# A later wait point for the second product of super-block 0 in a macaron transformer layer

## The chip, the cores and the metric

The kernel runs on one Trainium2 chip, on all 8 cores, each with its own batch element (2048 tokens of 1024 features) and the same weights. The metric is the device time in microseconds of the slowest core, from its first to its last instruction, as one launch takes it. The cores don't exchange data.

## What is computed

The layer is a feed-forward block, attention, and the same feed-forward block again, each with a layer normalisation in front and a residual around it:

```python
x = x + 0.5 * ffn(layernorm(x))
x = x + attn(layernorm(x))
x = x + 0.5 * ffn(layernorm(x))

def ffn(x):                       # n = tokens, D = 1024, HIDDEN = 4096
    top1 = argmax(softmax(x @ gate_w.T))        # one of two routed experts
    masked = x[None] * one_hot(top1)            # per expert, the others' tokens zeroed
    h = relu(einsum('end,edh->enh', masked, w1) + b1[:, None])
    routed = (einsum('enh,ehd->end', h, w2) + b2[:, None]).sum(0)
    return routed + relu(x @ sw1 + sb1) @ sw2 + sb2   # and the shared expert
```

Attention has 16 heads and uses one projection for query, key and value.

## The kernel before

`build` writes out, in Python, one list of instructions per engine, with semaphore waits made explicit by a small class `Sched`. `sch.bump(sem, n)` counts how far a semaphore will have come when everything emitted so far has run; `sch.val(sem)` is that count; `sch.wait(engine, sem, value)` puts a wait in the engine's list, and puts none if the value is 0 or if that engine has waited for as much already. Each engine then runs its list strictly in order. VectorE counts DVE, ScalarE counts ACTs, TensorE counts MM.

Three segments follow one another: `emit_ffn` (first feed-forward stage), `emit_attn`, and `emit_ffn` again. Activations lie in SBUF as `x_sb`, features on the partitions, and are worked on in 4 strips of 512 tokens (`NSTRIP`, `TS`). The hidden units of the shared expert and of the two routed ones, 3 x 4096, are cut into 12 super-blocks of 1024 (`NSUP`, `HE`): super-blocks 0 to 3 are the shared expert, 4 to 7 and 8 to 11 the routed ones, on masked input. The weights of a super-block are loaded by POOL's DMA queue two super-blocks ahead, once the block two before has ended (`issue_next`).

For each super-block and strip there are two products:

- `do_mm1` (L534): 8 groups of 8 matmuls, 128x128 weights by 128x512 activations, at L556, alternately into the PSUM banks ps_a and ps_b. ScalarE takes each out at L566 with bias and ReLU into `ar_h`.
- `do_mm2` (L582): 8 groups of 8 matmuls at L593, from `ar_h`, alternately into ps_c and ps_d. VectorE takes each out by adding it to the residual in `x_sb`: at L606 in super-block 0 (with the bias), at L613 in the others. Ahead of each group TensorE waits at L586 for the eviction that last used this bank (`ps2_free`) or for the argument `mm2_extra`, whichever is later.

Super-block 0 (L622 to L635) is interleaved with the layer normalisation of the coming strips, which the other super-blocks find finished:

- `stage_stats` (L314), called as `sf`: TensorE sums x (L326) and squares made by ScalarE (L344, L353); VectorE takes both rows out (L335, L361).
- `stage_post` (L366), called as `pf`: a few row operations (L373, L378, L385), a matmul that spreads the scale over the partitions (L391), ScalarE's exponential (L397), a matmul that spreads the mean (L402), and then 16 operations of VectorE, for each of 8 feature blocks a subtraction (L411) and a multiplication (L415), which write the normalised strip `ar_ln`.
- `stage_gate` (L423), called as `gf`: the routing masks (L435 to L477).

The order in which super-block 0 hands work to the engines is, for strips 0, 1, 2, 3: `do_mm1` of the strip, statistics of strip + 2, `pf` of strip + 1, `do_mm2` of the strip, and from strip 2 on the gate of strip - 2. So on VectorE the 16 operations for the next strip stand ahead of the 8 evictions of this strip's second product, and on TensorE the matmul of L402 stands directly ahead of L593. Strip 3 has neither statistics nor `pf` ahead of its second product.

`xwait_dve`, the argument of this call before, is 0 in the first stage and, in the second, the last VectorE count of attention, which TensorE waits for already ahead of the statistics.

Of the kernel before, what the change touches and what calls it, by code (L numbers as in the profile page):

```python
# [68 lines left out]
def build(phases=("ffn1", "attn", "ffn2")):  # L69
# [15 lines left out]
    with es:  # L85
# [40 lines left out]
        sch = Sched()  # L126
        X, MM, ACTs, DVE, GP, OUT = "x", "mm", "act", "dve", "gp", "out"
# [34 lines left out]
        def w2blk(slot, hc, dc):  # L162
            o = slot * 8192 + hc * 1024 + dc * 128
            return ar_w2[:, o:o + 128]
# [335 lines left out]
        def emit_ffn(xwait_dve, wst, ps_d, ps_w, ps_w2, ps_e, ps_f):  # L500
# [81 lines left out]
            def do_mm2(sup, st, slot, mm2_extra):  # L582
                h_all = max(h_relu_tok)
                for dc in range(NKC):
                    pst = (ps_c, ps_d)[dc % 2]
                    sch.wait("tensor", DVE, max(ps2_free[dc % 2], mm2_extra))  # L586
                    if dc > 0:
                        sch.wait("tensor", ACTs, h_all)
                    for hc in range(NKC):
                        if dc == 0:  # L590
                            sch.wait("tensor", ACTs, h_relu_tok[hc])
                        def f2(t, S, _hc=hc, _dc=dc, _slot=slot, _pst=pst):
                            ins = t.matmul(_pst[:, :], w2blk(_slot, _hc, _dc),  # L593
                                           ar_h[:, _hc * TS:(_hc + 1) * TS],
                                           start=(_hc == 0), stop=(_hc == NKC - 1))
                            if _hc == NKC - 1:
                                ins.then_inc(S[MM], 1)
                        sch.emit("tensor", f2)
                    g2 = sch.bump(MM, 1)
                    sch.wait("vector", MM, g2)  # L600
                    sch.wait("vector", DVE, tok_b2)
                    o0 = dc * NT + st * TS
                    if sup == 0:
                        def fx(v, S, _dc=dc, _o0=o0, _pst=pst):
                            xsl = x_sb[:, _o0:_o0 + TS]
                            v.scalar_tensor_tensor(  # L606
                                out=xsl, in0=_pst[:, :],
                                scalar=b2sh[:, _dc:_dc + 1], in1=xsl,
                                op0=ALU.add, op1=ALU.add).then_inc(S[DVE], 1)
                    else:  # L610
                        def fx(v, S, _o0=o0, _pst=pst):
                            xsl = x_sb[:, _o0:_o0 + TS]
                            v.tensor_add(xsl, xsl, _pst[:, :]).then_inc(S[DVE], 1)  # L613
                    sch.emit("vector", fx)
                    stt_tok[dc][st] = sch.bump(DVE, 1)
                    ps2_free[dc % 2] = stt_tok[dc][st]
                    if pending_lnm:
                        pending_lnm.pop(0)()
                while pending_lnm:
                    pending_lnm.pop(0)()  # L620

            sf[0](); sf[1](); pf[0]()  # L622
            for st in range(NSTRIP):
                do_mm1(0, st, 0, 0)
                if st + 2 < NSTRIP:
                    sf[st + 2]()
                if st + 1 < NSTRIP:
                    pf[st + 1]()
                do_mm2(0, st, 0, xwait_dve)
                if st == 2:  # L630
                    ext["all_ln"] = max(ln_tok)
                if st >= 2:
                    gf[st - 2]()
# [338 lines left out]
        if do1:  # L972
            with nc.psum_tensor("ps_d1", [128, TS], F32) as ps_d1, \
                 nc.psum_tensor("ps_w1", [1, TS], F32) as ps_w1, \
                 nc.psum_tensor("ps_v1", [1, TS], F32) as ps_v1, \
                 nc.psum_tensor("ps_e1", [128, TS], F32) as ps_e1, \
                 nc.psum_tensor("ps_f1", [128, TS], F32) as ps_f1:
                for s0 in range(2):
                    wst1["w1"][s0] = issue_w1(s0, s0 % 2, 0, "f1")
                    wst1["w2"][s0] = issue_w2(s0, s0 % 2, 0)  # L980

                def issue_next_ffn1(sup):
                    nxt = sup + 2
                    tok = wst1["sup_last_mm"][sup]
                    if nxt < NSUP:
                        wst1["w1"][nxt] = issue_w1(nxt, nxt % 2, tok, "f1")
                        wst1["w2"][nxt] = issue_w2(nxt, nxt % 2, tok)
                wst1["issue_next"] = issue_next_ffn1
                xw, _, ffn1_mm = emit_ffn(0, wst1, ps_d1, ps_w1, ps_v1, ps_e1, ps_f1)
                if doa:  # L990
                    wready["wq"] = issue_wqut("q", wst1["sup_last_mm"][10])
            sch.seg_break()
# [23 lines left out]
        if do2:  # L1016
            with nc.psum_tensor("ps_d2", [128, TS], F32) as ps_d2, \
                 nc.psum_tensor("ps_w2", [1, TS], F32) as ps_w2, \
                 nc.psum_tensor("ps_v2", [1, TS], F32) as ps_v2, \
                 nc.psum_tensor("ps_e2", [128, TS], F32) as ps_e2, \  # L1020
                 nc.psum_tensor("ps_f2", [128, TS], F32) as ps_f2:
                if wst2["w1"][0] is None:
                    wst2["w1"][0] = issue_w1(0, 0, attn_mm, "f2")
                wst2["w2"][0] = issue_w2(0, 0, attn_mm)
                wst2["w1"][1] = issue_w1(1, 1, attn_mm, "f2")
                wst2["w2"][1] = issue_w2(1, 1, attn_mm)

                def issue_next_ffn2(sup):
                    nxt = sup + 2
                    tok = wst2["sup_last_mm"][sup]  # L1030
                    if nxt < NSUP:
                        wst2["w1"][nxt] = issue_w1(nxt, nxt % 2, tok, "f2")
                        wst2["w2"][nxt] = issue_w2(nxt, nxt % 2, tok)
                wst2["issue_next"] = issue_next_ffn2
                _, xtok, _ = emit_ffn(xw, wst2, ps_d2, ps_w2, ps_v2, ps_e2, ps_f2)
# [97 lines left out]
```

## Time and profile before

| | us |
|---|---|
| two timed runs | 4184.4 and 4484.0, median 4334.2 |
| profiled execution, as timed | 4184.9 |
| its span (slowest core) | 4183.2 |
| spans of the eight cores | 4177.3 to 4183.2 |
| TensorE matmuls busy | 3810.0 (91%) |
| ScalarE busy | 1223.3 (29%) |
| VectorE busy | 1133.8 (27%) |
| POOL busy | 48.6 (1%) |

The two timed runs are 7% apart, so the profiled execution, close to the lower one, is the one to which the rows belong. The busy times are shares of a span made of unlike stages. The first feed-forward stage begins at about 50 us, when the input has landed; super-block 0 runs to about 296 us, attention from about 1540 to 2685, and super-block 0 of the second stage from there to about 2930.

### The profile page before, as it was taken

How to read it: one execution, taken by the hardware profiler on the slowest of the kernel's cores; microseconds unless marked ns; L12 is line 12 of the kernel's file. 1: busy time of each engine (PE TensorE's matmuls, PEld its weight loads, DVE VectorE, ACT ScalarE, POOL GpSimd, SP SyncE). 2: the span in 40 equal slices, each digit the busy share in tenths (PEclk: the TensorE clock that was granted, in tenths of full speed). 3: DMA queues.
4: the chain of work that ended last, by engine and by line, in shares of the span. 5: the costliest groups of instructions: out<-in, count | busy, mean ns of one | idle time of the engine just before them, and what ended most of it. 6: DMA issues, size and time to landing. Idle time of an engine off the chain costs nothing. (4 is left out here: it accounts for less than half of the span.)

```text
span 4183.2 us, 45422 instructions; the slowest of 8 cores (4177.3 to 4183.2 us)
## 1 busy us (share of the span) xinstructions
PE 3810.0 (91%) x16624; PEld 1598.7 (38%) x16880; DVE 1133.8 (27%) x2179; ACT 1223.3 (29%) x2956; POOL 48.6 (1%) x67
## 2 busy tenths in 40 slices
PE   3789999999999996889888889877999999999998
PEld 0234444444444431233332333323344444444443
DVE  1331212233223325121231212234211232233222
ACT  1111112111221121666637666421122112211121
POOL 0000000000000000000000000000000000000000
PEclk8899999999999997556575565789999999999999
DMA  7002222222222100100001000300222222222202
GB/s 161 0 1 41 41 41 41 41 41 41 41 41 41 21 1 0 21 1 1 1 1 21 1 1 1 45 16 0 41 41 41 41 41 41 41 41 41 36 6 81
DMA packets 55268, 124.63 MB, mean 30 GB/s; under 512 B 1808, under 2 KB 1808, under 8 KB 53008
## 3 DMA queue, kind: packets, MB, share of 16 engines
q0 software_dynamic: 52144, 104.86, 16.1%
q1 hardware_dynamic: 2912, 16.85, 1.2%
q8 instruction: 144, 2.36, 0.2%
q14 instruction: 68, 0.56, 0.0%
HBM read 218.18 MB, written 8.39 MB: 54 GB/s over the span
## 5 line engine op out<-in xcount | busy, mean ns | idle before, releaser
L566 ACT ACTIVATE ar_h<-ps_a,b1hf 128x512 bf16<-128x512 f32 x384 | 263.9, 687 | 1891.1 <-PE ps_a L556 1891.1
L593 PE MATMUL ps_c<-ar_h,ar_w 128*128 128x512 bf16 x3008 | 738.6, 386 | 54.5 <-DVE x_sb L606 50.5
L593 PE MATMUL ps_d<-ar_h,ar_w 128*128 128x512 bf16 x3010 | 722.3, 380 | 3.6 <-issue 0.4
L613 DVE TENSOR_TENSOR x_sb<-x_sb,ps_c 128x512 f32<-128x512 f32 x352 | 242.1, 688 | 1498.4 <-PE ps_c L593 1498.4
L556 PE MATMUL ps_a<-ar_b,ar_w 128*128 128x512 bf16 x2010 | 482.5, 379 | 4.8 <-DVE ar_b L522 2.6
L741 PE MATMUL s<-ar_h 64*128 64x512 bf16 x768 | 415.2, 567 | 73.7 <-ACT ar_w L752 51.5
L556 PE MATMUL ps_b<-ar_b,ar_w 128*128 128x512 bf16 x2004 | 479.5, 379 | 2.3
L593 PEld LDWEIGHTS ps_c<-ar_h,ar_w 128*128 128x128 bf16 x3072 | 303.4, 99 | 432.8 <-issue 81.5
L593 PEld LDWEIGHTS ps_d<-ar_h,ar_w 128*128 128x128 bf16 x3072 | 301.7, 98 | 368.2 <-issue 9.5
L566 ACT ACTIVATE ar_h<-ps_b,b1hf 128x512 bf16<-128x512 f32 x384 | 263.9, 687 | 401.1 <-PE ps_b L556 401.1
L752 ACT ACTIVATE ar_w<-s 128x512 bf16<-128x512 f32 x432 | 255.2, 598 | 308.6 <-PE s L741 307.1
L613 DVE TENSOR_TENSOR x_sb<-x_sb,ps_d 128x512 f32<-128x512 f32 x352 | 242.1, 688 | 283.1 <-PE ps_d L593 283.1
L556 PEld LDWEIGHTS ps_a<-ar_b,ar_w 128*128 128x128 bf16 x2048 | 200.4, 98 | 254.1 <-issue 21.9
L556 PEld LDWEIGHTS ps_b<-ar_b,ar_w 128*128 128x128 bf16 x2048 | 200.5, 98 | 234.4
L556 PE MATMUL ps_a<-ar_ln,ar_w 128*128 128x512 bf16 x994 | 244.8, 384 | 21.0 <-DVE ar_ln L415 19.0
L556 PE MATMUL ps_b<-ar_ln,ar_w 128*128 128x512 bf16 x1012 | 245.4, 384 | 0.6
L741 PEld LDWEIGHTS s<-ar_h 64*128 64x128 bf16 x768 | 75.0, 103 | 362.0 <-issue 361.6
L522 DVE TENSOR_TENSOR ar_b<-ar_ln,ar_b 128x512 bf16<-128x512 bf16 x512 | 213.1, 418 | 0.0
L556 PEld LDWEIGHTS ps_a<-ar_ln,ar_w 128*128 128x128 bf16 x1024 | 100.5, 98 | 148.9 <-issue 31.9
L741 PE MATMUL ps_t<-ar_h 64*128 64x512 bf16 x256 | 151.2, 590 | 4.5 <-ACT p_ex L752 0.4
L556 PEld LDWEIGHTS ps_b<-ar_ln,ar_w 128*128 128x128 bf16 x1024 | 101.3, 99 | 123.8 <-issue 5.9
L752 ACT ACTIVATE ar_ln<-s 128x512 bf16<-128x512 f32 x176 | 105.5, 615 | 43.7 <-PE s L741 43.7
(162 smaller groups left out, 2489.3 us busy)
## 6 DMA issues: line engine op xcount, KB each, us to landing
ar_w<-w1c POOLq DMA_DIRECT2D x24, 2048.0 KB, 18.3
ar_w<-w2c POOLq DMA_DIRECT2D x24, 2048.0 KB, 28.7
x_sb<-x SPq DMA_DIRECT2D x1, 8192.0 KB, 37.1
y<-x_sb SPq DMA_DIRECT2D x8, 1024.0 KB, 10.5
ar_w<-wqt POOLq DMA_DIRECT2D x1, 2048.0 KB, 16.4
ar_w<-wut POOLq DMA_DIRECT2D x1, 2048.0 KB, 17.0
b1hf<-b1h SPq DMA_DIRECT2D x1, 48.0 KB, 38.5
bq_sb<-bqc SPq DMA_DIRECT2D x1, 4.0 KB, 40.0
```

The costliest lines, as they stand in the source:

```text
L522: v.tensor_mul(lnm_ap(_kc), ln_ap(_kc, _st * TS, TS), mask_ap(_w, _st)).then_inc(S[DVE], 1)
L556: ins = t.matmul(_pst[:, :], w1blk(_slot, _kc, _hc), _rhs(_kc), start=(_kc == 0), stop=(_kc == NKC - 1))
L566: s.activation(ar_h[:, _hc * TS:(_hc + 1) * TS], _pst[:, :], AF.Relu, bias=b1hf[:, _sup * 8 + _hc:_sup * 8 + _hc + 1], scale=0.5).then_inc ...
L593: ins = t.matmul(_pst[:, :], w2blk(_slot, _hc, _dc), ar_h[:, _hc * TS:(_hc + 1) * TS], start=(_hc == 0), stop=(_hc == NKC - 1))
L613: v.tensor_add(xsl, xsl, _pst[:, :]).then_inc(S[DVE], 1)
L741: t.matmul(_sr[:, :], qq_ap(_pa, _h), ar_h[_h:_h + 64, _q4 * TS:(_q4 + 1) * TS], start=True, stop=True).then_inc(S[MM], 1)
L752: s.activation(prow_ap(_a)[:, _q4 * TS:(_q4 + 1) * TS], _sr[:, :], AF.Exp, scale=SCALE, accum_out=_z[:, _a * 4 + _q4:_a * 4 + _q4 + 1]).th ...
```

## The change

One argument of one call in `emit_ffn` is different. The second product of super-block 0 is called with the count of all that has been handed to VectorE when the call is made, instead of `xwait_dve`. The function is used by both feed-forward stages, so the call is made 8 times, once for each strip in each stage.

```diff
@@ -626,7 +626,7 @@
                     sf[st + 2]()
                 if st + 1 < NSTRIP:
                     pf[st + 1]()
-                do_mm2(0, st, 0, xwait_dve)
+                do_mm2(0, st, 0, sch.val(DVE))
                 if st == 2:
                     ext["all_ln"] = max(ln_tok)
                 if st >= 2:
```

## Rows read from the trace of the kernel before

**Rows 1.** Cores' spans and clocks; then the page's span and busy time.
```profile
core 6: 4180.6 us, clock 0.878
...
span 4183.2 us, 45422 instructions; the slowest of 8 cores (4177.3 to 4183.2 us)
...
PE 3810.0 (91%) x16624; PEld 1598.7 (38%) x16880; DVE 1133.8 (27%) x2179; ACT 1223.3 (29%) x2956; POOL 48.6 (1%) x67
```

**Rows 2.** TensorE's waits: who waited for whom, us in total, times, longest.
```profile
PE ps_c L593 <- DVE x_sb L606: 50.5, 6, 8.8
```

**Rows 3.** Timeline, strip 0, stage one: start, us, engine, line, operation [idle before <-releaser].
```profile
127.25 2.04 PE L402 MATMUL ps_f<-p_ex,onesLf 1*128 1x512 f32 x2 [0.84 <-ACT p_ex L397]
129.22 3.59 PE L593 MATMUL ps_c<-ar_h,ar_w 128*128 128x512 bf16 x8
129.54 0.69 DVE L411 TENSOR_TENSOR ar_ln<-x_sb,ps_f 128x512 bf16<-128x512 f32 x1 [6.04 <-PE ps_f L402]
...
141.44 0.69 DVE L415 TENSOR_TENSOR ar_ln<-ar_ln,p_ex 128x512 bf16<-128x512 bf16 x1
142.05 0.74 DVE L606 SCALAR_TENSOR_TENSOR x_sb<-ps_c,b2sh,x_sb 128x512 f32<-128x512 f32 x1
...
142.94 3.57 PE L593 MATMUL ps_c<-ar_h,ar_w 128*128 128x512 bf16 x8 [8.18 <-DVE x_sb L606]
...
146.31 2.13 PE L593 MATMUL ps_d<-ar_h,ar_w 128*128 128x512 bf16 x8
...
148.28 1.89 PE L593 MATMUL ps_c<-ar_h,ar_w 128*128 128x512 bf16 x8
148.55 0.75 DVE L606 SCALAR_TENSOR_TENSOR x_sb<-ps_d,b2sh,x_sb 128x512 f32<-128x512 f32 x1 [1.18 <-PE ps_d L593]
...
155.18 1.89 PE L556 MATMUL ps_a<-ar_ln,ar_w 128*128 128x512 bf16 x8
```

**Rows 4.** Timeline, strip 3, stage one: the gate's last eviction and the second product.
```profile
268.78 0.69 DVE L477 CAST ar_b<-ps_f 128x512 bf16<-128x512 f32 x1
...
281.63 1.89 PE L593 MATMUL ps_c<-ar_h,ar_w 128*128 128x512 bf16 x8
```

**Rows 5.** Timeline: an L415 that releases a matmul.
```profile
95.09 0.69 DVE L415 TENSOR_TENSOR ar_ln<-ar_ln,ar_b 128x512 bf16<-128x512 bf16 x1
...
95.93 0.58 PE L556 MATMUL ps_a<-ar_ln,ar_w 128*128 128x512 bf16 x1 [1.00 <-DVE ar_ln L415]
```

**Rows 6.** Stretches of 1 us: window and length, TensorE busy (x), granted clock, DMA, GB/s.
```profile
140.00:141.00 1.00, 0.00 (x0) 0.50 0.00 0
...
147.00:148.00 1.00, 1.00 (x6) 1.00 0.00 0
```

**Rows 7.** Timeline of TensorE: the longest and the shortest resumption, and where each ends.
```profile
202.22 3.57 PE L593 MATMUL ps_c<-ar_h,ar_w 128*128 128x512 bf16 x8 [8.80 <-DVE x_sb L606]
...
215.53 1.89 PE L556 MATMUL ps_a<-ar_ln,ar_w 128*128 128x512 bf16 x8
...
2837.09 3.26 PE L593 MATMUL ps_c<-ar_h,ar_w 128*128 128x512 bf16 x8 [8.69 <-DVE x_sb L606]
...
2848.82 1.89 PE L556 MATMUL ps_a<-ar_ln,ar_w 128*128 128x512 bf16 x8
```

**Rows 8.** Timeline: TensorE's first work after the initial load.
```profile
49.69 9.47 PE L326 MATMUL ps_w<-x_sb,ones_colf 128*1 128x512 f32 x16 [49.69 <-DVE b2sh L241]
...
53.91 0.13 PEld L326 LDWEIGHTS ps_w<-x_sb,ones_colf 128*1 128x1 f32 x1 [0.73 <-issue]
54.70 0.09 PEld L326 LDWEIGHTS ps_w<-x_sb,ones_colf 128*1 128x1 f32 x1 [0.66 <-issue]
55.13 0.08 PEld L326 LDWEIGHTS ps_w<-x_sb,ones_colf 128*1 128x1 f32 x1 [0.34 <-issue]
```

**Rows 9.** POOL's longest wait to 330 us; DMA issue, KB each, us to landing.
```profile
POOL ar_w L251 <- PE ps_f L467: 312.7, 1, 312.7
...
ar_w<-w2c POOLq DMA_DIRECT2D x1, 2048.0 KB, 29.0
```

## The prediction

> **What bounds the kernel now.** I read the spans of the cores first [rows 1]: the eight lie within 5.9 us (4177.3 to 4183.2), so no core or die stands out, and one core's trace can speak for all. TensorE is busy for 91% of the span [rows 1]; a change counts here by what it adds to TensorE's own line, or by the idle time it opens or closes on it. Next, the waits of TensorE [rows 2]: one of them is the wait this change is about. TensorE waited six times, 50.5 us in all and 8.8 us at the longest, for the eviction at L606 before it could write ps_c again at L593. Six is three strips in each of the two feed-forward stages. The third view is the timeline around the first of the six [rows 3], where the order of events is to be seen.
>
> At 127.25 us TensorE runs the last matmul of the normalisation of the next strip (L402). It ends at 129.29, and two things start side by side: VectorE's 16 operations of L411 and L415, from 129.54 to 142.13 (141.44 + 0.69), and on TensorE the first two groups of the second product, ps_c at 129.22 and ps_d, which end by about 134.8. The third group needs ps_c back. Its eviction (L606) stands on VectorE behind the 16 operations: it runs at 142.05, and the third group starts at 142.94. So VectorE's normalisation, not TensorE, sets when the third group starts. From there TensorE runs six groups without a gap to 155.18, where the next strip's first product begins. The two early groups lie wholly under VectorE's work: done by 134.8, they leave TensorE idle for 8.2 us.
>
> **The change, part by part.** The text replaces the value that TensorE waits for ahead of the second product in super-block 0. It was 0 in the first stage and the last tick of attention in the second, both long passed. It becomes the count of everything handed to VectorE up to there. The argument is worked out once per call, and a wait for a value already waited for is dropped, so each call gets one new wait, in front of its first group; the later groups wait for their own bank's eviction as before. There are 4 calls in each stage, 8 in all. No operation is added, removed or resized.
>
> *Strip 3, two calls: nothing.* No normalisation stands ahead of it. The last thing handed to VectorE is L477 of the gate, which starts at 268.78 and takes 0.69; the second product starts at 281.63 [rows 4], 12.2 us later. What covers the wait is the whole first product of the strip (14 us of TensorE); without that cover it would cost what is left of the gate's evictions, under 1.5 us.
>
> *Strips 0 to 2, six calls: the start.* The last thing handed over is L415 for kc = 7. Behind the waiting instruction in TensorE's queue stand all eight groups, and nothing else can pass. The first group now starts when L415 has ended, plus a hand-over. For this hand-over the trace has a row: L415 at 95.09 + 0.69 = 95.78 releases the matmul of L556 at 95.93 [rows 5], 0.15 us. Before, the *third* group started 0.81 us after the end of L415 (142.13 to 142.94: an eviction and its hand-over). So TensorE resumes 0.81 - 0.15 = 0.66 us sooner, but with eight groups to do instead of six.
>
> *The two groups.* A group at full clock takes 1.725 us from start to start (four from 148.28 to 155.18 [rows 3]). Two take 3.45 us. Per strip: 3.45 - 0.66 = 2.79 us.
>
> *The clock.* All six resumptions run at half clock for a while. In the first, the granted clock is 0.50 at 140, when TensorE has been idle for 5 us, and 1.00 again from 147 [rows 6]: the levels are 1.2 and 2.4 GHz. What this costs is the stretch from the resumption to the end of the sixth group, less 6 x 1.725 = 10.35: 155.18 - 142.94 = 12.24, so 1.89. The longest and the shortest of the six [rows 7] are, the same way, 215.53 - 202.22 = 13.31, so 2.96, and 2848.82 - 2837.09 = 11.73, so 1.38; the other three lie between. The mean of these three is 2.08. After the change TensorE is at half clock as well when it resumes, since it has been idle not for 8.2 but for 13.0 us (129.29 to 142.13 + 0.15). I take the same 2.08 on average and no difference: the nearest row for a longer idle, the start of the kernel, with its first matmul at 49.69, shows weight loads 0.79 us apart up to 54.70 and 0.43 apart after it [rows 8], so about 5 us at half clock, a cost of 2.5, inside the 1.38 to 2.96. The bounds are one of the two ends in all six: 6 x (1.38 - 2.08) = -4.2 us and 6 x (2.96 - 2.08) = +5.3 us. By the Trainium skill's "TensorE: Matmul & The Clock Gate", section "Part 1: The HAM clock gate", there are only two levels, idle brings the lower one and sustained work releases it, so that 13 us of idle leave the array no slower than 8 us; by it the clock adds nothing and the total is the one below, and the trace agrees: 0.50 after the short idle [rows 6], and weight loads at about twice the later spacing after the long one [rows 8].
>
> *Evictions after the resumption.* In the new order the first group's eviction no longer stands behind the normalisation. It takes 0.75 us and begins about 0.27 after the next group's start (148.28 and 148.55 [rows 3]); with the hand-over the bank is free 1.2 us into a group of at least 1.7. So the third group doesn't wait: nothing, as in all full-clock groups of before. VectorE's 16 operations keep their pace: from 129.54 to 141.44 they start 0.79 us apart on average, and each takes 0.69, the first beside a busy TensorE as well as the last beside an idle one [rows 3]: nothing. If the two evictions had no such cover, each would cost its 1.2.
>
> *What is late next.* The end of super-block 0 moves by 3 x 2.79 = 8.4 us, and with it POOL's issue of the weights for super-block 2 (it now waits 312.7 us for that point, and they land 29.0 us later [rows 9]). They are needed only after the whole of super-block 1, four strips of 64 + 64 matmul pairs, 4 x 16 x 1.725 = 110 us: hidden by 81. Attention and the output transfers shift as a whole.
>
> *Sum.* 6 x 2.79 = **16.7 us**. The profiled execution took 4184.9 us (span 4183.2 and 1.7 around it). It becomes 4184.9 + 16.7 = **4201.6 us**, +0.40%. The two timed runs were 4184.4 and 4484.0, with a median of 4334.2; my sum stands on the profiled execution, which agrees with the lower one, and the median is no run's time.
>
> **The rivals.**
>
> *The whole wait is new.* The new wait holds TensorE for the 13.0 us of normalisation, six times 78 us, and a clock that would have stayed up is lost too (6 x 2.08 = 12.5): 4184.9 + 78 + 12.5 = 4275 us, +2.2%. This is what the edit looks like in the text alone. It decides (slower by over 2%) from 84 us, 14 per strip. It needs that the third group not wait for VectorE today; it does [rows 2, 3], 8.2 us of idle time in the first case and 50.5 in six.
>
> *A longer slow stretch.* The longer idle keeps the clock down for so long that the two added groups run at 1.2 GHz on top of the slow stretch of today. A slow group takes 3.37 us (142.94 to 146.31 [rows 3]), so 2 x (3.37 - 1.725) = 3.3 more per strip, 20 in six: 4221 us. Against it stands the start of the kernel, where a far longer idle was followed by 5 us of slow clock, not 7.
>
> *It does nothing.* The wait is passed already or dropped: 4184.9. It is true of strip 3. For strips 0 to 2 VectorE would have to be done before TensorE gets there; it starts its 16 operations only after the matmul that stands directly ahead of the second product.
>
> *VectorE gets faster with TensorE quiet.* If the 16 operations each ended 0.175 us sooner, the 2.79 us would be gained back and the time is 4185; with more it would be faster than before. The 0.69 of the last operation, with TensorE idle for 6 us, is that of the first and speaks against it.
>
> **How the numbers follow.** My forecast has a chance of 0.86; a longer slow stretch 0.05; does nothing 0.03; VectorE faster 0.02 (half of it a small gain, within 2%); the whole wait 0.03; 0.01 for anything else that makes it faster by over 2%. The forecast's own bounds are 16.7 - 4.2 = 12.5 and 16.7 + 5.3 = 22.0: 4197 to 4207. The slowest core adds to that: it was 2.6 us behind the next and 5.9 behind the first of the cores [rows 1], which another execution may not repeat, or may exceed by as much; I allow 5 either way, so 4192 to 4212. I give **4191 to 4214**, a little beyond. The main case and nearly nothing of the others lies in it. Two per cent is 84 us, about what a measurement of this kernel can tell from no change: faster 0.01, within it 0.96, slower 0.03.
>
> **What would show it.** In the profile of the changed kernel: TensorE's wait at ps_c L593 is no longer for L606 but for L415 of ar_ln, six times, 78 us in all and about 13 each; the matmuls of ps_c and ps_d start together about 0.15 us after the last L415, with no idle time between the eight groups; the stretch from the last L415 to the next strip's first product is 16.0 us on average (0.15 + 13.8 + 2.08) where it is 13.05 in strip 0 of before; VectorE idles 3 to 4 us before its first L606 of each strip; the strip 3 stretch and everything from super-block 1 on are unchanged but for the shift. I would be wrong if the idle row stayed near 50, if the slow stretch after the resumption ran over 6 us, or if the groups between showed waits for L606.

## The result, and the profile after

| | before | after |
|---|---|---|
| median of all executions | 4409.2 (12) | 4269.7 (15) |
| lowest | 4181.2 | 4208.1 |
| ratio | | 1.0064 (95% interval 1.0048 to 1.0080) |
| spans in the profile, of the cores that are read | 4177.3 to 4183.2 (all) | 4202.7 to 4205.2 (cores 0 to 3) |

The change makes the kernel slower by 0.64%, some 26 us. In 9 of the 12 executions of before and in half of those of after, the cores of one die or both show a lower clock and end 60 to 560 us late, so the two medians say nothing of the change, and the ratio and all stretches below are of executions and cores without it. The eight executions of after in the ratio lie between 4208.1 and 4210.7.

The spans of the cores answer [rows 1]. The traces of after are read on core 2.

```profile
die 0 (median of its cores): 4203.9 us, clock 0.873
```

The waits of TensorE (us in total, times, longest) answer [rows 2]. The wait for L606 is gone, and one for L415 stands in its place.

```profile
PE ps_c L593 <- DVE ar_ln L415: 78.3, 6, 13.4
```

The timeline of strip 0 on core 2 answers [rows 3]: start, us, engine, line, operation, idle before it.

```profile
127.06 2.04 PE L402 MATMUL ps_f<-p_ex,onesLf 1*128 1x512 f32 x2 [0.84 <-ACT p_ex L397]
...
141.25 0.69 DVE L415 TENSOR_TENSOR ar_ln<-ar_ln,p_ex 128x512 bf16<-128x512 bf16 x1
142.09 3.57 PE L593 MATMUL ps_c<-ar_h,ar_w 128*128 128x512 bf16 x8 [12.99 <-DVE ar_ln L415]
145.46 2.45 PE L593 MATMUL ps_d<-ar_h,ar_w 128*128 128x512 bf16 x8
145.78 0.75 DVE L606 SCALAR_TENSOR_TENSOR x_sb<-ps_c,b2sh,x_sb 128x512 f32<-128x512 f32 x1 [3.84 <-PE ps_c L593]
...
158.10 1.89 PE L556 MATMUL ps_a<-ar_ln,ar_w 128*128 128x512 bf16 x8
```

All eight groups follow the wait. L415 ends at 141.94, TensorE starts 0.15 us later, and the next strip's first product starts at 158.10, 16.16 us after L415, where it was 13.05 in [rows 3].

**Where the 26 us are.** The marks are the first starts and last starts of four lines in the timeline: L326, L606, L613 and the score matmuls of attention. Between them, in us, the median over cores (before: cores 1 to 7; after: cores 0 to 3). Core 0 of before is left out since its stage one reads otherwise (246.0, 45.0 and 138.6 in the first, second and fourth line); with it no median moves by over 0.1.

| stretch | before | after | difference |
|---|---|---|---|
| stage one, super-block 0 (first L326 to last L606) | 243.7 | 252.8 | +9.1 |
| stage one, gates (last L606 to first L613) | 42.6 | 45.1 | +2.5 |
| stage one, the rest of the super-blocks | 1204.0 | 1204.0 | 0 |
| attention: normalisation and query | 140.1 | 138.6 | -1.5 |
| attention: scores | 976.5 | 975.9 | -0.6 |
| stage two, super-block 0 | 240.9 | 250.7 | +9.8 |
| stage two, gates | 39.2 | 45.2 | +6.0 |
| stage two, the rest | 1202.3 | 1202.3 | 0 |

Together +25.3, against 25.5 between the medians of the spans (4178.4 and 4203.9). Of this, 18.9 us lie in super-block 0, where 16.7 were forecast, and 8.5 in the stretch called gates, where nothing was. That stretch holds the routing masks (L435 to L477) of strips 1, 2 and 3, which come between the last second product of super-block 0 and super-block 1, and the whole first product of super-block 1's first strip. The order and the number of its instructions are the same in both kernels.

The windows view over just this stretch, stage two, on core 2 (length, TensorE busy, granted clock, DMA, GB/s), the kernel before first:

```profile
2921.50:2960.80 39.30, 29.91 (x128) 0.96 0.38 55
```
```profile
2940.50:2985.80 45.30, 35.91 (x128) 0.81 0.39 57
```

And the timeline of TensorE in it. Before:

```profile
2929.00 3.18 PE L435 MATMUL ps_e<-ar_ln,gw_bf 128*1 128x512 bf16 x8 [0.94 <-DVE ar_b L475]
...
2938.33 1.89 PE L435 MATMUL ps_e<-ar_ln,gw_bf 128*1 128x512 bf16 x8 [0.94 <-DVE ar_b L475]
...
2944.97 1.90 PE L556 MATMUL ps_a<-ar_ln,ar_w 128*128 128x512 bf16 x8
```

After:

```profile
2947.94 2.64 PE L435 MATMUL ps_e<-ar_ln,gw_bf 128*1 128x512 bf16 x8 [0.94 <-DVE ar_b L475]
...
2957.69 3.57 PE L435 MATMUL ps_e<-ar_ln,gw_bf 128*1 128x512 bf16 x8 [0.94 <-DVE ar_b L475]
...
2967.14 3.59 PE L556 MATMUL ps_a<-ar_ln,ar_w 128*128 128x512 bf16 x8
2970.53 3.02 PE L556 MATMUL ps_b<-ar_ln,ar_w 128*128 128x512 bf16 x8
```

The idle stretches between the groups are the same (0.94 ahead of L435 in both, and 2.50 ahead of L465). What differs is how much of the stretch TensorE runs at 1.2 GHz: the same eight matmuls take 1.89 or 3.57 us. The first product of super-block 1, at full clock in before, begins with two slow groups in after.

### The profile page after: what moved, and what is told of

It is laid out like the page before. It is cut to its first block and busy times, and to the rows that moved or that the text cites. A ratio compares the mean times of both kernels' runs of the same rounds, so it can differ in the third digit from the quotient of the medians.

```text
span 4268.1 us, 45422 instructions; the slowest of 8 cores (4202.7 to 4268.1 us)
## 1 busy us (share of the span) xinstructions
PE 3865.7 (91%) x16624; PEld 1610.4 (38%) x16880; DVE 1134.8 (27%) x2179; ACT 1222.4 (29%) x2956; POOL 48.6 (1%) x67
## 5 line engine op out<-in xcount | busy, mean ns | idle before, releaser
L593 PE MATMUL ps_c<-ar_h,ar_w 128*128 128x512 bf16 x3008 | 742.0, 388 | 82.2 <-DVE ar_ln L415 78.3
L593 PE MATMUL ps_d<-ar_h,ar_w 128*128 128x512 bf16 x3010 | 735.2, 385 | 3.8 <-issue 0.4
L613 DVE TENSOR_TENSOR x_sb<-x_sb,ps_c 128x512 f32<-128x512 f32 x352 | 242.0, 688 | 1525.0 <-PE ps_c L593 1525.0
L613 DVE TENSOR_TENSOR x_sb<-x_sb,ps_d 128x512 f32<-128x512 f32 x352 | 242.0, 688 | 290.7 <-PE ps_d L593 290.7
L556 PE MATMUL ps_a<-ar_ln,ar_w 128*128 128x512 bf16 x994 | 262.2, 404 | 21.6 <-DVE ar_ln L415 19.0
L556 PE MATMUL ps_b<-ar_ln,ar_w 128*128 128x512 bf16 x1012 | 261.7, 403 | 0.7
## 6 DMA issues: line engine op xcount, KB each, us to landing
ar_w<-wut POOLq DMA_DIRECT2D x1, 2048.0 KB, 14.6
b1hf<-b1h SPq DMA_DIRECT2D x1, 48.0 KB, 39.9
```

What stands on the lines that cost most here:

```text
L556: ins = t.matmul(_pst[:, :], w1blk(_slot, _kc, _hc), _rhs(_kc), start=(_kc == 0), stop=(_kc == NKC - 1))
L593: ins = t.matmul(_pst[:, :], w2blk(_slot, _hc, _dc), ar_h[:, _hc * TS:(_hc + 1) * TS], start=(_hc == 0), stop=(_hc == NKC - 1))
```

## The experiments

My theory after this reading: each held strip costs the two groups that were under VectorE's normalisation, a little more half-clock time at its resumption, and, by way of *when* the gates come, half-clock time in them. The rivals: the gates' time is chance; it comes of the absolute time of arrival or of the weights' transfers beside it; it comes of the longer idle time itself. The edits are shown shortened. I give the lowest time of each kernel, beside that of the kernel before on the same chip, and judge by the stretches above.

### The new wait in one stage

```diff
-                do_mm2(0, st, 0, xwait_dve)
+                do_mm2(0, st, 0, sch.val(DVE) if xwait_dve == 0 else xwait_dve)
```

> The new wait is kept in the first feed-forward stage alone. My theory: the change costs (a) 3.1 to 3.4 us for each held strip, two groups of matmuls that used to run under VectorE's normalisation, and (b) half-clock time in the gate work that follows super-block 0, which depends on what TensorE did in the same stage. Then stage one reads as in the changed kernel (super-block 0 252.6, gate 45.1) and stage two as in the kernel before (240.9 and 39.2), attention 1.5 to 2.5 us shorter as in the changed kernel: 4184 + 9.5 + 2.5 - 2.5 = 4193 to 4196. Rival, the gate time is chance or is set by the absolute time of arrival: then stage two's gate moves away from 39.2 although nothing in stage two was edited.

Measured: lowest 4191.8 (before 4181.0). On cores 0, 1 and 4 to 7 stage one reads 252.4 to 255.0 in super-block 0 and 45.1 to 45.2 in the gates, attention's first part 138.6, and stage two 240.8 to 241.2 and 39.2 to 39.3, as in the kernel before.

```diff
+                do_mm2(0, st, 0, sch.val(DVE) if xwait_dve > 0 else xwait_dve)
```

> The new wait is kept in the second feed-forward stage alone. My theory: stage one as before (243.2 and 42.6), attention as before (140.1), stage two as in the changed kernel (super-block 0 250.7, gate 45.2): 4184 + 9.8 + 6.0 = 4200. Together with the stage-one kernel the parts add up to the whole within 2 us. Rival, chance or absolute time: the gate of stage two reads something else than 45.2.

Measured: lowest 4196.6, against 4181.0, as expected within the spread. The two kernels cost 10.8 and 15.6 us, together 26.4, as the whole change does. Stage two reads 250.5 to 250.9 and 45.2 to 45.3 on all eight cores. Stage one has 42.6 in the gates on seven cores. The eighth is core 1, with 45.0. It belongs together with core 0 of the kernel before, which also has 45.0 in its stage one, and both then have 138.6 in attention's first part, where the cores with 42.6 have 139.9 to 140.2.

The gates of a stage follow what was done in the same stage, whenever that stage arrives (stage two comes 10 us later in the first kernel, and its gates don't move). So absolute time is out. Pure chance is out for stage two, where the value repeats to 0.1 us over all eight cores. In stage one two cores without any held strip read 45.0, so there the value alone shows less. What sets them apart is small. From TensorE's last resumption in super-block 0 to the last eviction (L606) they need 46.8 us, and the cores that read 42.6 need 46.4 to 46.6. The two marks on core 0 of the kernel before:

```profile
248.93 1.87 PE L593 MATMUL ps_c<-ar_h,ar_w 128*128 128x512 bf16 x4 [8.44 <-DVE x_sb L606]
...
295.72 0.75 DVE L606 SCALAR_TENSOR_TENSOR x_sb<-ps_d,b2sh,x_sb 128x512 f32<-128x512 f32 x1 [0.98 <-PE ps_d L593]
```

In stage two of before the same distance is 46.6 to 46.7 us, and the gates read 39.2.

### The new wait in strip 2 alone

```diff
+                do_mm2(0, st, 0, sch.val(DVE) if st == 2 else xwait_dve)
```

> The new wait is kept for strip 2 alone, the last strip ahead of the gate work, in both stages. My theory: super-block 0 grows by 3.3 us in each stage instead of 9.5. If the gate's half-clock time hangs on the last resumption before it, the gates read 45 in both stages and the total is 4184 + 6.6 + 8.5 = 4199; if it hangs on the delay of all three strips together, the gates read something between 39 and 45 in each, and the total is 4184 + 6.6 + 0 to 8.5.

Measured: lowest 4200.2; the cores other than 2 and 3 end at 4186.9 to 4194.6. Stage two reads 243.9 to 244.3 in super-block 0, 3.2 us over before for one strip, and 45.1 in the gates on all eight cores; stage one has 44.9 to 45.2 there. One held strip, the last ahead of the gates, brings the whole of the gates' loss, so that the other two aren't needed for it. That is the first branch of the expectation.

### The gates shifted without any wait

```diff
+                if sup == 0 and st == 3:
+                    sch.wait("tensor", DVE, ps2_free[0])
+                    for k in range(8):   # one extra group into ps_c, overwritten
```

> The kernel before, with 8 extra matmuls (one group, 1.73 us at full clock) ahead of the second product of strip 3, in both stages; no wait is touched and no idle time is opened. It tests what sets the half-clock time in the gates. If it is set by when the gates come, counted from the last resumption, the gate stretches leave 42.6 and 39.2 for other values between 37.7 and 47, though the work in them is the same. If it is set by the 13 us of idle time or by the new wait, they stay at 42.6 and 39.2. Super-block 0 grows by 1.7 us in each stage either way.

Measured: 4199.5, the lower of two executions (before 4186.0). Super-block 0 of stage two reads 242.5 to 242.9 (+1.7, the group), and the gates 46.4 to 47.5, in stage one 46.3 to 47.5. Cores 2 and 3, whose granted clock is 1.00 or 0.50 throughout, have 46.4 in stage two, and 46.3 and 46.5 in stage one. Here the gates on core 2, the window from the last eviction on:

```profile
2923.80:2970.30 46.50, 37.11 (x128) 0.78 0.39 69
```

So a group of 1.73 us in the middle of continuous work, with no wait and no idle time opened, costs 7 us more in the gates of stage two and 4 in stage one. The wait and the 13 us of idle time aren't needed for it: what has moved is when the gates come after the last resumption. The value doesn't grow with that distance. Sorted by it, both stages taken together, the gates read 42.6 (46.4 to 46.6 us), 39.2 (46.6 to 46.7), 45.0 (46.8), 46.3 and more (48.1 to 48.5, this kernel) and 44.9 to 45.3 (50.2 to 50.6, the held strips). So the 8.5 us are no price of the wait as such: a shift of a tenth or two decides between values that lie 3 to 6 us apart.

### The gates filled

Twelve matmuls of the gate's own form go where TensorE waits for the masks' rows:

```diff
+                for k in range(12):
+                    t.matmul(statps[1], gw_bf[:, 0:1], ln_ap(_k % 8, _t0, TS),
+                             start=True, stop=True)
                 sch.wait("tensor", DVE, mrow_tok)
```

> The kernel before, with 12 extra matmuls (128x1 by 128x512, into the unused statistics bank) in each gate, in the 2.7 us in which TensorE waits for the masks' rows. If the gate's excess is half-clock time that the short idle stretches bring on, it goes away: the gate stretch reads 37 to 38 us in both stages, where the kernel before has 42.6 and 39.2. If it is something else (the weights' transfers that run beside it), it stays at 42.6 and 39.2.

> The changed kernel with the same 12 extra matmuls in each gate. If the clock in the gates is what the changed kernel loses beyond its held strips, the gate stretch reads the same as in the kernel before with this fill (37 to 38) in both stages, and the two filled kernels differ by 17 us (2 x 9.6 in super-block 0, less 2 in attention) instead of 26. If the gates stay apart by 2.5 and 6.0 us, the clock is not the cause.

Measured: 4176.3 for the kernel before with the fill (before 4180.2) and 4196.3 for the changed one. The gates read 37.7 us in both kernels, both stages, on every core, at a clock of 1.00. The filled kernel before, then the filled changed kernel, core 2, stage two:

```profile
2914.30:2952.00 37.70, 35.60 (x162) 1.00 0.34 51
```
```profile
2933.80:2971.50 37.70, 35.60 (x162) 1.00 0.39 59
```

The gates' excess was half-clock time and nothing else; the weights' transfers ran beside them here too. With it out, the two kernels differ by 20.0 us, not 26 to 27, and so do their stretches: 10.0 in super-block 0 of stage one, 9.8 in that of stage two, 0.2 in attention's first part (cores 0 to 3 and 0 to 5). The 17 expected took off 2 us for attention, which isn't there: on these cores both filled kernels read 138.6 to 138.9 in its first part. Without that credit 2 x 9.6 = 19.2 were to be expected, and it is about what is left: the price of the six held strips.

### The idle time filled

```diff
+                    for k in range(46):   # ahead of the new wait, strips 0 to 2
+                        t.matmul(ps_c[:, :], w2blk(0, _k % 8, 0),
+                                 ln_ap(_k % 8, _st * TS, TS), start=True, stop=True)
```

> The changed kernel, with 46 extra matmuls (128x128 by 128x512, into ps_c, overwritten later) in front of the new wait in strips 0 to 2, so that TensorE works through nearly all of the 13 us. It separates the two groups from the clock. My theory: TensorE resumes at full clock, each held strip costs 3.45 - 0.66 = 2.8 us for the two groups, less the 1.3 to 3.0 us of half clock that the resumption of the kernel before pays, so super-block 0 reads 245 to 247 in stage one and 243 to 245 in stage two, where the changed kernel has 252.6 and 250.7. Rival, the slow resumption has nothing to do with idle TensorE: super-block 0 stays at 252 and 250. The gate after it may read anything from 39 to 45, since the last change of the clock before it now lies elsewhere.

Measured: 4197.8 (before 4180.2). The timeline of TensorE in strip 0, core 2:

```profile
134.12 8.70 PE L587 MATMUL ps_c<-ar_ln,ar_w 128*128 128x512 bf16 x37 [0.22 <-issue]
143.37 1.89 PE L600 MATMUL ps_c<-ar_h,ar_w 128*128 128x512 bf16 x8 [0.55 <-DVE ar_ln L415]
...
157.18 1.89 PE L556 MATMUL ps_a<-ar_ln,ar_w 128*128 128x512 bf16 x8
```

After the wait the eight groups take 157.18 - 143.37 = 13.81 us, 8 x 1.726: no slow stretch. In the changed kernel they took 16.01. So a resumption's loss is half-clock time that idle TensorE brings. But super-block 0 reads 244.4 only on cores 6 and 7, in stage two; cores 0 to 3 have 247.2 to 247.4 there, where 243 to 245 were expected, and all eight have 248.4 to 250.7 in stage one, where it was 245 to 247. On core 2 part of it comes back elsewhere: the strip 2 matmuls of L391 and L402 take 1.45 and 2.04 us where core 6 has 1.09 and 1.09, and the first group of strip 3 takes 3.11 where core 6 has 1.90. The half-clock time moved.

### The wait one group later

```diff
+                    sch.wait("tensor", DVE, max(ps2_free[dc % 2],
+                                                mm2_extra if dc > 0 else 0))
```

> The new wait stands one group later, ahead of the second group instead of the first, in both stages; the first group runs under VectorE's normalisation again. If the groups that are no longer covered are the cost, one group of 1.73 us comes back per strip, and seven follow the wait: 7 x 1.725 + 0.15 against 6 x 1.725 + 0.81 is 1.07 per strip, 6.4 us in six, plus what the clock does in the gates (0 to 8.5): 4190 to 4199. If instead the length of TensorE's idle time (11.3 us here, 13.0 in the changed kernel, 8.2 before) were the cost, most of the 26 us would stay, at 4203 or more.

> The wait ahead of the second group once more, for a profile: per strip one group less than in the changed kernel follows the wait, so super-block 0 reads 240.9 + 3 x 1.07 = 244 to 246 in stage two (250.7 in the changed kernel, 240.9 before), 246 to 249 in stage one. The gates may read anything from 38 to 47.

Measured: lowest 4198.2 on the first chip (before 4181.0), 4204.7 in two executions on another (before 4186.0). TensorE idles 9.5 to 10.1 us and not 11.3, since the first group runs at half clock. It is between before and after. In the trace of the second chip super-block 0 reads 247.7 to 248.1 in stage two, where 244 to 246 were expected, and 249.7 to 252.2 in stage one, where it was 246 to 249; the gates read 42.6 to 43.9 and 39.9 to 47.2. The groups account for 3.2 of the 7.0 us. The rest is half-clock time again: the three resumptions lose 1.99, 2.58 and 1.53 us on core 0 (6.1; 5.0 on core 2 of before), and more stands in strip 2's L402 and strip 3's first groups. The loss doesn't follow the length of the idle time: strip 1's resumption in stage two loses 1.3 us after 8.7 us of it, 2.6 after 9.5, and 1.8 after 13.0. My expectation left the clock of super-block 0 out, the error of the prediction once more.

### The opposite order

The 16 operations of the next strip are no longer ahead of the evictions but two after each:

```diff
-                    pf[st + 1]()
+                    pf[st + 1](pending_lnm)   # stage_post puts its 8 blocks there;
                 do_mm2(0, st, 0, xwait_dve)   # do_mm2 runs one after each eviction
```

> The opposite of the change: the 16 normalising operations of the next strip are no longer ahead of the eight evictions on VectorE but go between them, two after each eviction. If the kernel before is held by evictions that stand behind the normalisation, TensorE no longer waits 8.2 to 8.8 us for L606; VectorE sets the pace with 0.75 + 2 x 0.79 = 2.3 us for a group, and the next strip's first product can start as the blocks appear, 5 us sooner per strip: 243.2 and 240.9 become 226 to 230 and 224 to 228, the total 4184 - 30 = 4150 to 4158. If the order does not matter because VectorE has the same work anyway, the total stays within 5 us of 4184.

Measured: 4165.6 (before 4180.2), 14.6 us less, half of what I expected. The waits of TensorE, core 2:

```profile
PE ps_a L561 <- DVE ar_ln L416: 29.1, 22, 3.5
...
PE ps_d L598 <- DVE x_sb L611: 4.3, 12, 0.4
PE ps_c L598 <- DVE x_sb L611: 2.5, 8, 0.4
```

The wait for the evictions shrinks from 50.5 us to 6.8, and super-block 0 of stage two from 240.9 to 230.5. Two things were missed: TensorE waits for the last two blocks of the next strip (0.66 and 1.87 us each time), and the gates went to 45.0 or 45.9 in stage one and 45.1 in stage two, a loss of 2.4 to 3.4 and 5.8 us against before. That this has the same cause as above is tried next.

The same kernel with the gates filled, by the edit shown above:

```diff
+                for k in range(12):   # ahead of the wait for mrow_tok
+                    t.matmul(statps[1], gw_bf[:, 0:1], ln_ap(_k % 8, _t0, TS), ...)
```

> The interleaved order (two normalising operations after each eviction) together with the 12 extra matmuls in each gate. If the two are independent, super-block 0 reads as in the interleaved kernel (231 to 234 and 230.5) and the gates as in the filled kernels (37.7 twice, instead of 45.0): 7.3 us less in each stage than the interleaved kernel's 4165.6, so 4151. If the half-clock time only moves elsewhere when it is taken out of the gates, the total stays above 4160.

Measured: 4149.6 (before 4186.0), ratio 0.9928 (0.9900 to 0.9956), where 4151 were expected if the two edits are independent. The gates read 37.7 to 39.2, and super-block 0 of stage two 228.8. No stretch at 0.50 is left in the gates. What some cores have over 37.7 is a third level of the granted clock, which core 2 shows in stage one with TensorE busy all the time:

```profile
313.00:318.00 5.00, 5.00 (x21) 0.81 1.12 150
```

In the last one, which keeps that fill, the first two blocks come ahead of the first eviction, where VectorE was idle:

```diff
-                    if defer is None:
+                    if defer is None or kc < 2:
```

> As the kernel above, but the first two of the eight normalised blocks come ahead of the first eviction, where VectorE is idle while TensorE works on the first groups; the other six follow the evictions. The stalls of TensorE for the last two blocks (0.66 and 1.87 us for each strip in the interleaved kernel) should go: 2.5 us in each of six strips, 15 in all, so 4136. If VectorE is the bound over the whole strip and not only at its end, or the eviction held back by two blocks stalls the third group again, less than 6 us are gained.

Measured: 4129.6 (before 4186.0), ratio 0.9885 (0.9825 to 0.9944); super-block 0 219.3 to 221.5 and 217.5, against 243.7 and 240.9. It gained 20 us over the kernel above, more than the 15 of the two stalls; what gave the further 5 isn't shown. Of TensorE's waits for L416 only those of the very first strip of each stage are left, as they were in before (17.8 us, 16 times):

```profile
PE ps_a L567 <- DVE ar_ln L416: 17.8, 16, 1.9
```

It beats both kernels: its lowest time is 56 us below before, 1.3%.

## Why the prediction was right or wrong

- **The wait that goes and the one that comes: right.** 78 us in six were forecast and 78.3 measured, with L415 as the releaser, 0.15 us from its end to the first group, no wait between groups.
- **The two groups, 2.79 us per strip: right.** With the clock held up by the fill of the idle time the eight groups take 13.81 us, as in the sum. 16.7 and the 2.8 of the clock at the resumptions, below, make 19.5; the two kernels with filled gates differ by 20.0.
- **Strip 3's wait, VectorE's pace, the evictions, the prefetch: right.** The rest of either stage is unchanged to 0.1 us, and VectorE's operations take 0.69 us as before.
- **The clock at the resumptions: the mechanism right, the term mis-sized.** I took no difference. On core 2, stage two, the three resumptions of before lose 2.0, 1.3 and 1.6 us, those of after 2.4, 1.9 and 2.2: 1.5 more in this stage and 1.3 in stage one, 2.8 in all where the term was nothing. With the 8.4 of the groups that is 9.9 in stage two, and 9.8 was measured. The bound of +5.3 us in six holds it. The level was the same after 8 and 13 us of idle time, 0.50, as forecast; that this makes the loss the same doesn't follow. That there are two levels only holds in the trace of before; other traces show 0.81 as a third.
- **The step that failed: the sum ends at the resumption, and all that comes behind it was put at nothing.** "everything from super-block 1 on are unchanged but for the shift" and "attention and the output transfers shift as a whole" treat later work as a block that moves. The gates do not: with the same work and the same idle stretches they took 2.5 and 6.0 us longer. The experiments settled it: it is half-clock time (filled, it is gone), it needs no wait (the padded strip), and one held strip, the last, is enough for all of it (strip 2 alone). The size, +8.5, could not have been read off the rows as a cost: it is where the shift happened to put the gates. Attention gave 2.1 back, perhaps in the same way, which was only seen and not tried. So +26 us stand where +16.7 were forecast, 0.64% where 0.40% were.
- **The rivals.** The whole wait as new (+90 us) and no effect at all are both out. The longer slow stretch, priced at 20 us more, named the right subject, the clock, but the wrong place: at the resumptions it was 2.8 us in all, and the rest of the missing time lay in the gates.
- **The range** of 4191 to 4214 was built for one-sided errors of the clock at the resumption and the spread of cores. The eight executions of the ratio (4208.1 to 4210.7) lie in it by luck: the allowance for cores and clock happened to cover the gates. The median over all, 4269.7, does not. The range was built on the profiled execution alone, though one of the two timed runs of before stood at 4484.0.

## What to carry to other kernels

A wait put earlier costs the work that it takes out from under the other engine, and not its own length: 78 us of waiting, where 50 were waited already, cost 20. Where TensorE works in short bursts with gaps of one to three us, as in the gates here, its clock depended on when they came, so that a shift ahead of them added several us; look at the granted clock of such stretches before you call them unchanged. Filling the gap with throw-away matmuls made them steady here, and taking evictions out from behind a long block of other work on the same engine gained more than the change had cost.

## What the runs showed of the hardware

- The same stretch of gates took 37.7 (filled), 39.2, 42.6, 45.1 or 46.5 us, with TensorE's granted clock at 1.00, 0.96, 0.88, 0.81 and 0.78 over it. In stage two the value repeats over the cores to 0.1 us, and one extra group of 1.73 us ahead of it moved it by 4 us in stage one and 7 in stage two. It goes with the distance from TensorE's last resumption, and 0.1 to 0.2 us of that distance are enough to change it.
- Attention's first part goes with what came before it, with 1204 us of matmuls between. In the kernel before and in the one with the new wait in stage two alone, cores whose stage one had 42.6 us in the gates had 139.9 to 140.2 us there, and those with 45.0 had 138.6. It is no fixed pairing: with the idle time filled, core 5 had 42.4 and 138.6, and with the gates filled 37.7 went with 138.6 to 138.9. Why is open.
- Taking half-clock time out at one place can bring it back at another: with the 13 us gap filled, strip 3's first group took 3.11 us on one core and 1.90 on another.
- A granted clock of 0.81 stands beside 1.00 and 0.50 in some traces, also while TensorE works without a pause and its neighbours in time are at 1.00.
